# Attention stage of a two-layer graph kernel: softmax sums per group of edges, merged into planes of state on VectorE

## What is computed

```python
x_l = (x @ W_l.T + b_l).reshape(n, H, C)            # H = 4, C = 32
x_r = (x @ W_r.T + b_r).reshape(n, H, C)
z = leaky_relu(x_l[src] + x_r[dst], 0.2)            # edges, and a loop at every node
e = einsum('ehc,hc->eh', z, att)
m = segment_max(e, dst)                             # per node and head
e = exp(e - m[dst])
denom = segment_sum(e, dst)
alpha = e / (denom[dst] + 1e-16)
out = segment_sum(alpha[:, :, None] * x_l[src], dst)
```

## Time and profile before

| | us |
|---|---|
| median of 3 runs | 4523.22 (4513.04 to 4539.57) |
| profiled execution | 4527.14 |
| its span in the profile | 4525.3 |
| TensorE clock granted, mean over the span | 0.801 of full |

### The profile page before, as it was taken

How to read it: one execution, slowest core, us unless ns; L and a number is a source line. 1 busy time by engine, 2 the same in 40 slices (tenths; PEclk the granted TensorE clock), 3 DMA queues, 4 the chain that set the end, 5 groups by cost and what they waited for, 6 DMA issues and landing times. The chain is left out here.

```text
span 4525.3 us, 110910 instructions
## 1 busy us (share of the span) xinstructions
PE 3323.5 (73%) x21794; PEld 2607.9 (58%) x21794; DVE 2389.8 (53%) x8999; ACT 1666.1 (37%) x3873; POOL 2996.9 (66%) x3168
## 2 busy tenths in 40 slices
PE   3487878878788888788656777777777777777771
PEld 2376666666666666666324565555555555555551
DVE  4233333333333333333455777777777777777776
ACT  2222222222222222222343454444444444554442
POOL 0377777777777777777006777777777777777760
PEclk8667676677766666766877999999998999999985
DMA  3555545545555554544123333333333333333330
GB/s 98 143 137 137 134 137 133 137 135 136 135 136 133 137 135 136 136 135 100 29 67 83 81 83 82 84 81 82 84 83 80 82 83 83 82 83 83 84 72 29
DMA packets 490579, 465.02 MB, mean 103 GB/s; under 512 B 242732, under 2 KB 389258, under 8 KB 490306
## 3 DMA queue, kind: packets, MB, share of 16 engines
q1 hardware_dynamic: 386978, 256.04, 22.1%
q0 software_dynamic: 100352, 205.72, 18.3%
q10 hardware_dynamic: 2976, 0.92, 0.1%
HBM read 436.00 MB, written 26.30 MB: 102 GB/s over the span
## 5 line engine op out<-in xcount | busy, mean ns | idle before, releaser
L613 POOL DMA_INDIRECT t_got<-tab_l,t_idx x1568 | 1485.8, 948 | 556.9 <-issue 461.9
L613 POOL DMA_INDIRECT m_got<-tab_a,m_idx x1568 | 1489.3, 950 | 501.6 <-issue 477.9
L850 PE MATMUL bank<-w,m_attr_t 128*128 128x128 f32 x3136 | 843.6, 403 | 1.0
L934 DVE TENSOR_TENSOR m_pre<-bank,m_got 128x512 f32<-128x512 f32 x392 | 271.2, 692 | 1073.7 <-DMA m_got<-tab_a,m_idx 1045.2
L893 ACT ACTIVATE m_hid<-m_pre 128x512 f32<-128x512 f32 x392 | 246.9, 630 | 1463.6 <-DVE m_pre L934 1454.3
L850 PEld LDWEIGHTS bank<-w,m_attr_t 128*128 128x128 f32 x3136 | 724.1, 284 | 61.9 <-issue 8.9
L1458 PE MATMUL bank<-t_hot_t,t_win 96*128 96x128 bf16 x1568 | 315.7, 232 | 355.9 <-DMA t_got<-tab_l,t_idx 341.7
L1475 PEld LDWEIGHTS bank<-t_a_edge,t_got 128*128 128x128 f32 x3136 | 444.9, 204 | 221.7 <-issue 221.6
L1500 ACT ACTIVATE t_z<-bank 128x512 f32<-128x512 f32 x392 | 234.0, 597 | 864.9 <-PE bank L1460 686.7
L860 PE MATMUL bank<-m_hid,m_hot 128*32 128x129 f32 x3136 | 211.4, 348 | 368.0 <-ACT m_part L899 338.6
L1467 PE MATMUL bank<-t_zt,att_w 128*128 128x512 f32 x784 | 461.0, 674 | 0.0
(11 more groups left out here) (188 smaller groups left out, 5335.4 us busy)
## 6 DMA issues: line engine op xcount, KB each, us to landing
m_attr_in<-in_edge_attr_dram SPq DMA_DIRECT2D x390, 256.0 KB
m_row<-dst_rows SPq DMA_DIRECT2D x392, 128.0 KB
t_row<-dst_rows SPq DMA_DIRECT2D x392, 128.0 KB
m_got<-tab_a,m_idx POOLq DMA_INDIRECT x1568
t_got<-tab_l,t_idx POOLq DMA_INDIRECT x1568
t_win<-tab_r SPq DMA_DIRECT2D x1176, 8.0 KB
m_win<-tab_b SPq DMA_DIRECT2D x392, 24.0 KB
t_self_in<-tab_es SPq DMA_DIRECT2D x392, 0.5 KB
```

The lines of the kernel that those rows point to most:

```text
L613: pool.indirect_dma_start(out=r.got[u][:, j, :], out_offset=None, in_=table, in_offset=bass.IndirectOffsetOnAxis(ap=r.idx[half][:, i, j:j ...
L850: pe.matmul(p_hid[q % 2][:, e], lhsT=attr_t[q % 2][:, e], rhs=k.w1[:, 2, :], start=True, stop=False)
L934: dve.tensor_tensor(pre[q % 2][:], p_hid[q % 2][:], r.got[q][:].rearrange("p j d -> p (j d)"), ALU.add).then_inc(s["m_sum"], 1)
```

## The change

Per group and head, maximum, exponentials and sums are now taken within the group alone (the logits come out negated, by `att_wn`, so that the maximum is a minimum). The state is a plane of negated maxima per node `top_n` (it lies in `HT`, free by then, and starts with the loops' own logits, which `nodes_middle` now leaves there for all 128 partitions) beside the two planes of sums in `acc`. A group is merged six slots later: DVE takes the difference between group and state (`gap`), updates the state (`min`), makes two exponents (`drop`), ACT turns both into factors in one instruction (`shrink`, 128x64), and DVE scales old and new sums and adds them (`old`, `new`, `sums`). The carried maximum, the shift matrix, their matmul on PE and the setup of their tables go.

On PE the weighted sums are made in four column strips of 32: 16 small products per group in place of 4 large ones. The order of the steps in a slot is another on PE, ACT and DVE. SP issues two loads per group in place of five, the window by one transfer of 96 rows of 256 bytes out of a table whose rows hold all three parts. DVE puts the indices out in slots 0 and 4 of a round, behind `zt`, where it was slots 3 and 7; at the start of the stage it does so before it clears `acc`, where it was after.

```diff
+        dve.tensor_scalar(k.att_wn[:], k.same_head[:], k.att[:, 0:1], -1.0, ALU.mult, ALU.mult)
...
-                    last = pe.matmul(k.bank[b][0:H, 0:HALF], lhsT=k.att4[:], rhs=zt[:, cols], start=True,
+                    last = pe.matmul(k.bank[b][:, 0:HALF], lhsT=k.att_wn[:], rhs=zt[:, cols], start=True,
...
             hold(sp, s["b_es"], l + 1)
-            sp.dma_start(k.tab_es[:, bass.ds(l * N2, N2)], es[:]).then_inc(s["b_out"], 16)
+            sp.dma_start(k.tab_es[:, bass.ds(l * N2, N2)],
+                         k.HT[0:P:W, bass.ds(l * N2, N2)]
+                         ).then_inc(s["b_out"], 16)
             hold(sp, s["b_lrow"], l + 1)
             hold(sp, s["b_lo"], l + 1)
-            store_tables(sp, s, k, s["b_out"], l * N2, [(k.tab_l, lrow[:]), (k.tab_r, rrow[:])],
-                         [(k.tab_r3, [b[:] for b in r3])])
-        sp.wait_ge(s["b_out"], k.NI * 16 * 6)
+            store_tables(sp, s["b_out"], l * N2, [(k.tab_l, lrow[:]), (k.tab_r, rrow[:])])
+            sp.dma_start(k.tab_r3[bass.ds(l * N2, N2), :, :].rearrange("(t p) c d -> p t c d", p=P), r3[:]
+                         ).then_inc(s["b_out"], 16)
+        sp.wait_ge(s["b_out"], k.NI * 16 * 4)
...
     def load(sp, g, u):
         sp.dma_start(r.row[u][:], k.dst_rows[bass.ds(g, 1), :].to_broadcast([P, EG])).then_inc(r.s_in[u], 16)
         n0 = sp.value_load(k.base_i[0:1, bass.ds(g, 1)], min_val=0, max_val=k.NP - W)
-        for part in range(3):
-            sp.dma_start(r.win[u][part * W:(part + 1) * W, :], k.tab_r3[part, bass.ds(n0, W), :]
-                         ).then_inc(r.s_in[u], 16)
-        with nc.allow_non_contiguous_dma(reason="one logit on each partition"):
-            sp.dma_start(self_in[u][:], k.tab_es[:, bass.ds(n0, W)]).then_inc(r.s_in[u], 16)
+        sp.dma_start(r.win[u][:], k.tab_r3[bass.ds(n0, W), :, :].rearrange("w c d -> c w d")
+                     ).then_inc(r.s_in[u], 16)
...
-            hold(sp, s["t_mold"], g + 1 - U)
             hold(sp, s["t_zp"], g + 1 - U)
             load(sp, g, u)
...
+        if at := before(rnd, u, 5, tail):
             g, q = at[0] * U + at[1], at[1]
...
+            hold(pe, s["t_at"], g + 1)
+            hold(pe, s["t_cd"], g + 1)
+            hold(pe, s["t_acc"], g - 1)
+            for j in range(J):
+                for h in range(H):
+                    own = slice(h * W, (h + 1) * W)
+                    pe.matmul(p_nd[q % 2][own, 0:W], lhsT=r.got[q][:, j, own],
+                              rhs=a_edge[q % 2][:, j, own], start=(j == 0), stop=(j == J - 1),
+                              tile_position=(0, h * W))
+            pe.matmul(p_nd[q % 2][:, W:3 * W], lhsT=k.same_head[:],
+                      rhs=cd[q % 2][:].rearrange("p a w -> p (a w)"), start=True, stop=True
+                      ).then_inc(s["t_ndp"], 1)
...
         if at := before(rnd, u, 4, tail):
...
+        if at := before(rnd, u, 2, tail):
+            g, q = at[0] * U + at[1], at[1]
+            hold(pe, s["t_z"], g + 1)
+            hold(pe, s["t_mg"], g - 1)
+            pe.matmul(p_e[q % 2][:], lhsT=k.att_wn[:], rhs=zt[q % 2][:], start=True, stop=True
+                      ).then_inc(s["t_ep"], 1)
         if at := before(rnd, u, 1, tail):
             g, q = at[0] * U + at[1], at[1]
...
+            after(act, s["t_drop"], g + 1)
+            after(act, s["t_acc"], g - 1)
+            act.activation(shrink[q % 2][:], drop[q % 2][:], ACT.Exp).then_inc(s["t_s"], 1)
+        if at := before(rnd, u, 3, tail):
             g, q = at[0] * U + at[1], at[1]
...
+            after(act, s["t_mg"], g + 1)
+            after(act, s["t_turned"], g - 1)
+            act.activation(a_row[q % 2][:], logit[q % 2][:], ACT.Exp, scale=-1.0,
+                           bias=den_max[q % 4][:, 1:2], accum_out=den_max[q % 4][:, 0:1]
+                           ).then_inc(s["t_a"], 1)
         if at := before(rnd, u, 4, tail):
             g, q = at[0] * U + at[1], at[1]
             after(act, s["t_turned"], g + 1)
             after(act, s["t_ndp"], g - 1)
             act.activation(a_edge[q % 2][:].rearrange("p j c -> p (j c)"), p_turn[:], ACT.Copy
                            ).then_inc(s["t_at"], 1)
...
+        if at := before(rnd, u, 1, tail):
             g, q = at[0] * U + at[1], at[1]
...
+            after(act, s["t_masks"], g + 1)
+            after(act, s["t_mg"], g - 3)
+            act.activation(pen[q % 4][:], hot_t[q % 2][:], ACT.Identity, bias=big[:, 0:1],
+                           scale=-BIG).then_inc(s["t_pen"], 1)
+            after(act, s["t_zp"], g + 1)
+            after(act, s["t_z"], g - 1)
+            act.activation(z02[q % 2][:], p_z[q % 2][:], ACT.Copy, scale=SLOPE
+                           ).then_inc(s["t_z02"], 1)
+rounds(act, NR, body, 6)
...
-    dve.memset(k.acc[:, 1, :], 1.0)
-    dve.memset(negbig[:], -BIG)
-    dve.memset(prev[:], 1.0).then_inc(s["t_ones"], 1)
     for half in range(2):
         stage_indices(dve, k, r, half * (U // 2), half)
+    dve.memset(big[:], BIG)
+    dve.memset(k.acc[:, 1, :], 1.0).then_inc(s["t_ones"], 1)
     dve.wait_ge(s["t_ones"], 1)
     def body(rnd, slots, tail):
         for u in slots:
-            now = None if tail else rnd * U + u
-            third, sixth = before(rnd, u, 3, tail), before(rnd, u, 6, tail)
+            sixth = before(rnd, u, 6, tail)
...
+            top_w = top_n[:, bass.ds(n0, W)]
             hold(dve, s["t_ndp"], g + 1)
...
+            dve.tensor_tensor(gap[:], p_nd[q % 2][:, 2 * W:3 * W], top_w, ALU.subtract
+                              ).then_inc(s["t_gap"], 1)
+            dve.tensor_tensor(top_w, p_nd[q % 2][:, 2 * W:3 * W], top_w, ALU.min)
+            hold(dve, s["t_gap"], g + 1)
+            hold(dve, s["t_s"], g - 1)
+            dve.tensor_scalar(drop[q % 2][:, 0, :], gap[:], 0.0, None, ALU.min)
+            dve.tensor_scalar(drop[q % 2][:, 1, :], gap[:], -1.0, 0.0, ALU.mult, ALU.min
+                              ).then_inc(s["t_drop"], 1)
+        if at := before(rnd, u, 3, tail):
+            g, q = at[0] * U + at[1], at[1]
             hold(dve, s["t_pen"], g + 1)
             hold(dve, s["t_ep"], g + 1)
             hold(dve, s["t_a"], g - 1)
             dve.tensor_tensor_reduce(out=logit[q % 2][:], in0=p_e[q % 2][:], in1=pen[q % 4][:],
...
+                                     scale=1.0, scalar=3.0e38, op0=ALU.add, op1=ALU.min,
+                                     accum_out=den_max[q % 4][:, 1:2]).then_inc(s["t_mg"], 1)
         if at := before(rnd, u, 4, tail):
             g, q = at[0] * U + at[1], at[1]
...
+            hold(dve, s["t_a"], g + 1)
             hold(dve, s["t_ndp"], g - 1)
             dve.tensor_tensor(cd[q % 2][:], k.diag_w[:].unsqueeze(1).to_broadcast([P, 2, W]),
...
+                              den_max[q % 4][:].unsqueeze(2).to_broadcast([P, 2, W]), ALU.mult
                               ).then_inc(s["t_cd"], 1)
...
+        if not tail:
+            g = rnd * U + u
+            hold(dve, r.s_in[u], n_in * (rnd + 1))
+            hold(dve, s["t_zp"], g - 1)
+            hold(dve, s["t_pen"], g - 1)
+            dve.tensor_scalar(hot_t[u % 2][:], r.row[u][:], k.win_id[:, bass.ds(g, 1)], None,
+                              ALU.is_equal).then_inc(s["t_masks"], 1)
         if sixth:
             g, q = sixth[0] * U + sixth[1], sixth[1]
...
+            sums = k.acc[:, :, bass.ds(n0, W)]
+            hold(dve, s["t_s"], g + 1)
+            dve.tensor_tensor(old[:], sums, shrink[q % 2][:, 0, :].unsqueeze(1)
+                              .to_broadcast([P, 2, W]), ALU.mult)
+            dve.tensor_tensor(new[:], p_nd[q % 2][:, 0:2 * W].rearrange("p (a w) -> p a w", a=2),
+                              shrink[q % 2][:, 1, :].unsqueeze(1).to_broadcast([P, 2, W]),
+                              ALU.mult).then_inc(s["t_scaled"], 1)
+            hold(dve, s["t_scaled"], g + 1)
+            dve.tensor_tensor(sums, old[:], new[:], ALU.add).then_inc(s["t_acc"], 1)
         if at := before(rnd, u, 1, tail):
             g, q = at[0] * U + at[1], at[1]
             hold(dve, s["t_ep"], g - 1)
             hold(dve, s["t_z02"], g + 1)
             dve.tensor_tensor(zt[q % 2][:], p_z[q % 2][:], z02[q % 2][:], ALU.max
                               ).then_inc(s["t_z"], 1)
+            if q % (U // 2) == U // 2 - 1:
+                stage_indices(dve, k, r, g + 1 + U // 2, q // (U // 2))
 rounds(dve, NR, body, 6)
```

More of the change, by code:

```diff
@@ L135, in gnn_program @@
         k.X = sb("X", [P, NT, P], F32)
[L136 removed]
+        k.HT = sb("HT", [P, NP], F32)
         k.acc = sb("acc", [P, 2, NP], F32)
@@ L992, in nodes_middle @@
         r1 = sb("b_rest", [P, NTB, P])
-        r3 = [sb(f"b_part{q}", [P, NTB, P], BF16) for q in range(3)]
+        r3 = sb("b_part", [P, NTB, 3, P], BF16)
         def tile_of(first, q):
@@ L1229, in edges_attention @@
         r = edge_slots(ctx, nc, sems, "t")
```

(40 more changed lines are left out.)

141 lines of the change are left out of this document (25 added, 116 removed).

## The result

| | before | after |
|---|---|---|
| median of 8 runs, us | 4520.65 (4505.9 to 4539.57) | 4554.28 (4550.39 to 4556.76) |
| profiled execution: span, us | 4525.3 | 4548.6 |
| TensorE clock granted over the span | 0.801 | 0.777 |
| first `zt` of the attention stage, us | 2399.05 | 2386.20 |
| last `zt`, us | 4412.09 | 4437.66 |

The ratio is 1.0068 (95% interval 1.0055 to 1.0081): the changed kernel is slower by 0.7%, 34 us by the medians. The last three lines of the table say where it goes, for the two profiled executions. Up to the first `zt` the change gains 12.9 us, between the first and the last it loses 38.4, and behind the last it gains 2.3; the sum, a loss of 23.3, is the difference of the two spans. The other ten us lie in the choice of the executions: the profiled one of the change (4550.39) is the fastest of its eight, the one before (4527.14) stands 6.5 above its median.

A forecast was written before the change was run, and what follows sets the result against it. POOL's four gathers per group were taken as the bound, DVE close behind; after the change, a DVE-ACT loop about level. 4527 + 12 - 5 - 1 = 4533 profiled, 4 above the median: 4529 us, range 4480 to 4685.

The forecast's parts named there:

- within 0.5%: Whole kernel: about 22.6 us either way, 4500.6 to 4545.8, can't be told from no change; chance 0.42.
- slower: Whole kernel: time above the no-change band, by a DVE round-end stall or a longer DVE-ACT loop; chance 0.38.
- case A: Attention stage: DVE-ACT loop and POOL's gathers level, 5.10 to 5.22 us per group, 4500 to 4545; the forecast, chance 0.42.
- case D: Attention stage: instruction fetches go, but the DVE-ACT loop takes 5.3 to 5.4 us, giving 4600; chance 0.15.
- POOL's floor: Attention stage: POOL's gathers can't go below 1974 us, 41 less than before.
- the ring: Attention stage: one-slot loop over DVE and ACT, `t_z` round to `t_z`; terms sum to 5.00 us, estimate 5.00 to 5.30.
- a round of 41.35: Attention stage: 5.17 us per group, against 41.1 per round before; 49 x 0.25 = +12 us.
- ACT's new order: ACT's slot: 0.2 z now stands behind the exponentials, which closes a one-slot loop with DVE, summing to 5.00 us.
- Indices: Put out in slots 0 and 4: POOL's 0.95 us wait per round goes; gain up to 41 us, here 0.
- The round's end on DVE: 287 instructions in place of 400: the 3.45 us stall per round falls to a few tenths.
- The 32 passes of a strip product: PE's weighted sums: 0.4 to 1.44 us, taken as 0.7; nothing on the time at full clock.
- Once: Stage start and `nodes_middle`: -5.3 us as `acc`'s memset leaves the first gather's path, -1 for fewer stores.

The follow-up runs named there:

- the ring shortened: Changed kernel with logits ahead of the merge's small steps on DVE and `shrink` behind the exponentials on ACT: 4458.81 us, ratio to before 0.9834.
- the disturbed pace: Nine runs, of variants of both kernels, beside which the kernel before took 6690 to 6880 us in place of 4520.

## Why the prediction was right or wrong

The time, 4554, lies in the range of 4480 to 4685 and 25 us from the 4529 forecast. It moved past the 0.5% that was taken for no change (4545.8), so the likeliest case "within 0.5%" is not what came; "slower" had 0.38. The time fell in the gap between case A (to 4545) and case D (4600); by its mechanism it is A's ring, a little longer. That the forecast is only 25 off has luck in it: the stage lost 26 us more than the sum had, and what happens once gave back 9 more. (The other 8 us are where the two profiled executions stand against their medians: 4 above was reckoned with, 3.9 below came.)

**The bound.** POOL's floor was read right: with the ring shortened the stage runs at 40.1 us per round, and POOL waits for another engine twice. The estimate of the floor, 1974 us, compares with 1484.2 + 477.2 = 1961 measured.

**The ring.** Right in mechanism, and in most of its terms. By the slot shown above, predicted and measured: `t_z` to `zt` 0.63 and 0.73, `zt` to `gap` 0.85 and 0.94, `gap` to `t_logit` 1.0 and 0.90, `t_logit` to `t_a_row` 0.73 and 0.74, then 0.70 and 0.72, 0.48 and 0.48, 0.61 and 0.61. Two terms were 0.1 too small and one was 0.1 too large; the sum 5.00 came out as 5.12. That the ring bounds was argued ahead of the result and shown by the run that takes the merge's steps out.

**What was mis-sized** is the step from that sum to "a round of 41.35": it came out as 42.0. 0.8 of a round are the 0.1 by which each slot is longer. For the copies and the round's end I had 1.35 in all and they took 1.2 (0.16 for one copy; 0.81 across the round's end and 0.22 in the slot after it). `zt` to `zt` "5.1 to 5.2 in every slot, also across a round's end" missed the latter: 5.9. So "+12" for the stage was +38.

**Why this order** was told half. The prediction blamed ACT's new order, 0.2 z behind the exponentials. Putting 0.2 z ahead again gave 5107: in the changed kernel that closes a longer ring, through PE. What the ring could do without were the small steps of the merge, which stand ahead of `t_logit` on DVE and, through `shrink`, ahead of the exponentials on ACT: about 0.7 us, by the estimate of 4.4 for the ring without them (POOL bounds at 5.0 there, so the 4.4 itself wasn't measured).

**Indices.** "POOL's wait of 0.95 per round goes" was wrong. It still waits 35 times within rounds, 44.6 us:

```profile
3432.01 0.95 POOL L602 DMA_INDIRECT t_got<-tab_l,t_idx  x1 [1.45 <-DVE t_idx L589]
3434.64 0.95 POOL L602 DMA_INDIRECT t_got<-tab_l,t_idx  x1 [1.69 <-issue]
```

The copies come behind `zt`, and `zt` comes late by the ring; they are put out when DVE gets to them. With the ring shortened, they wait no more (two waits, 21.6 us, of which 21.3 where the stage starts). I had written that the gain would not show while the ring bounds; the name of the wait stayed too.

**The round's end on DVE.** Right: no stall with 287 instructions, and a stall with the same instructions 58 further along. By pieces of 128 instructions a body of 287 touches three or four, as its start falls. The prediction took three and didn't ask where the body starts; that it was right here was in part luck, and the moved body shows the other outcome. The Trainium skill (Runtime: NRT & Kernel Launch, Instruction fetch mechanics) has a store of 32 KiB, which four pieces of 8.2 KB fit. Its blocks of 16 KiB and its rule that the target of a taken branch must lie in the two pages at hand, read as the prediction reads them, would have kept the stall in the changed kernel, and the measurement decides: 7 packets.

**PE.** The 32 passes of a strip product, from start to the next group:

```profile
3434.79 0.46 PE L1431 MATMUL bank<-t_a_edge,t_got 128*32 128x32 f32 x32 [0.69 <-ACT t_a_edge L1490]
3435.18 0.32 PE L1434 MATMUL bank<-t_cd,same_head 128*128 128x64 f32 x1
```

0.39 us from start to start at a granted clock of 1.00, the end of the bounds that goes by columns; I had taken 0.7. Nothing hangs on it here: PE is not in the ring.

**Once.** The indices ahead of the memset: first index copy to first gather 0.6 us, against 5.7 from the memset's start before, so -5.1 for the -5.3 predicted. The rest of the 13.1 by which the first gather is earlier stands ahead of the stage, where DVE starts 8.1 earlier (2376.1 and 2384.2). Setup gives 1.7 of them (it no longer makes the shift table, which I left out of the sum); by the first gather of the MLP stage it is 3.2, by the first product of `nodes_middle` 4.4, and the remaining 3.7 fall in that block and its stores, where I had 1.

So in the sum: stage +38 for +12, once -15 for -6 (12.9 ahead of the first `zt` and 2.3 behind the last), together 23 for 6.

## What to carry to other kernels

When an edit takes work off engines that aren't the bound, list the loops that cross engines from one slot to the next and sum them start to start from the rows. Here the sum of seven terms was within 0.12 us of what came, while the busy times (DVE 347 us less) pointed the wrong way. Then look which steps in the ring don't need to be in it: this change became 1.7% faster than the kernel before by moving the merge behind the step that the ring needs, on both engines. Where a loop's body lies in its engine's instructions can be worth more than all of that: check the packets of the instruction queue after an edit. And moving a step to the other side of one engine's slot can close a longer ring through a third engine; sum that one too.

## What the hardware showed that I had not expected

- 58 instructions put ahead of a loop, 1.9 us of work, cost 181 us: the same body, moved by that much, came with 243 packets of 8.2 KB in place of 7, five a round, and 3.85 us more at each round's end.
- PE's granted clock from 2400 to 4300 us was 0.95 with the shortened ring, 0.87 in the changed kernel, 0.83 with the body moved and 0.73 with the order on ACT changed, on the same instructions of PE. The slower the stage, the lower the clock; where PE is in the ring, as in the last, that makes it slower again. Why the clock falls with the pace wasn't tried.
- At the disturbed pace ACT stood waiting for 6.7 us after PE's product was there while POOL issued gathers, and the order of steps in a slot hardly mattered (6236 to 6345 us in five runs of three kernels).
